# Cross-attention and mixture-of-experts kernel: operands over two queues, constants ahead, norms, weight pieces and first FFN chunks at other units

## What is computed

```
x = x + xattn(layernorm(x), ctx_1024)         # 16 heads of 8, causal mask, softmax
x = x + ffn(layernorm(x))                     # exact gelu
# xattn: q = Q @ Wq.T + bq, k and v from the context; w = softmax(mask(q @ k.T / sqrt(8)));
#        (w @ v) @ Wo.T + bo
# ffn:   shared experts (2 of 64) plus 16 routed experts of 64, top 4 of softmax(x @ router.T),
#        each gelu(x @ up.T) scaled by its gate, times down
```

## Time and profile before

| | us |
|---|---|
| median of 3 runs | 219.24 |
| lowest and highest of them | 218.1 and 220.63 |
| the profiled execution's own time | 219.43 |
| its span, first to last instruction | 217.7 |
| TensorE busy | 187.0 (86%) |
| VectorE busy | 170.6 (78%) |
| ScalarE busy | 143.4 (66%) |
| GpSimd busy | 97.1 (45%) |

### The profile page before, as it was taken

One profiled execution on the slowest core, in us unless ns is written; L12 is line 12 of the kernel. 1 busy time (PEld: TensorE's weight loads), 2 busy tenths in 40 slices (PEclk: granted clock), 3 DMA queues, 4 the chain that ended last, 5 costly groups with the idle time before them and its releaser, 6 DMA issues.

```text
span 217.7 us, 4911 instructions
## 1 busy us (share of the span) xinstructions
PE 187.0 (86%) x1610; PEld 137.3 (63%) x1610; DVE 170.6 (78%) x456; ACT 143.4 (66%) x285; POOL 97.1 (45%) x184
## 2 busy tenths in 40 slices
PE   0538689959999899999999997879959989999992
PEld 0316465646777577677767774457848758787871
DVE  4589969829689989999899994237788597787881
ACT  2261267746697687776766778866868977668661
POOL 5789018929569666566474666711112000000000
PEclk9999999996999999999999999999999999999999
DMA  4524332651332312312313200100000010010011
GB/s 121 168 62 121 77 102 78 212 155 52 93 87 51 103 56 63 106 39 77 79 53 81 74 5 5 32 6 24 3 2 0 5 50 0 0 48 0 9 41 48
DMA packets 23736, 12.98 MB, mean 60 GB/s; under 512 B 4696, under 2 KB 23400, under 8 KB 23712
## 3 DMA queue, kind: packets, MB, share of 16 engines
q1 hardware_dynamic: 23040, 12.52, 20.9%
q10 hardware_dynamic: 576, 0.13, 0.3%
q0 software_dynamic: 96, 0.03, 0.1%
HBM read 3.86 MB, written 1.05 MB: 23 GB/s over the span
## 4 chain that ended last, share of the span: by engine, by line
PE 50%; DVE 20%; issue 9%; SPq 8%; ACT 6%; DMA 3%; POOL 2%; POOLq 0%; DVEq 0%; ACTq 0%
DVE sb_mx L774 8%; SPq L335 6%; PE psum L964 6%; PE psum L946 4%; PE psum L883 3%; PE psum L880 3%; PE psum L881 3%; PE psum L923 3%; PE psum L865 3%; PE psum L867 3%; PE psum L866 3%; DVE sb_qk_res L757 2%; PE psum L872 2%; PE psum L967 2%; PE psum L930 2%
## 5 line engine op out<-in xcount | busy, mean ns | idle before, releaser
L774 DVE TENSOR_REDUCE sb_mx<-psum 128x2 f32<-128x512 f32 (+1 forms) x96 | 63.0, 679 | 8.0 <-PE psum L930 5.3
L582 ACT ACTIVATE sb_probs<-psum 128x512 f32<-128x512 f32 x96 | 55.9, 603 | 18.9 <-PE psum L946 18.0
L428 POOL TENSOR_SCALAR_AFFINE_SELECT sb_probs<-sb_probs 128x256 f32<-128x256 f32 (+1 forms) x96 | 45.1, 484 | 35.0 <-ACT sb_probs L582 34.4
L665 DVE TENSOR_TENSOR sb_probs<-sb_probs,psum 128x512 f32<-128x512 f32 x32 | 21.9, 684 | 10.1 <-ACT sb_probs L526 9.8
L526 ACT ACTIVATE sb_probs<-psum 128x512 f32<-128x512 f32 x36 | 21.4, 599 | 12.1 <-PE psum L867 12.0
L946 PE MATMUL psum<-sb_qk_op 128*128 128x256 bf16 x128 | 24.6, 274 | 3.1 <-ACT sb_probs L582 3.0
L923 PE MATMUL psum<-sb_qk_op 96*128 96x256 bf16 x128 | 25.9, 285 | 0.0
L672 DVE TENSOR_TENSOR sb_hid_l<-sb_probs,sb_hid_h 128x512 fp32r<-128x512 f32 x36 | 24.7, 685 | 0.3
L532 ACT CAST sb_hid_h<-sb_probs 128x512 fp32r<-128x512 f32 x36 | 22.2, 616 | 2.9 <-DVE sb_probs L665 2.9
L920 PE MATMUL psum<-sb_fut,sb_id_b 128*128 128x256 bf16 x64 | 18.3, 286 | 5.2 <-issue 4.4
L964 PE MATMUL psum<-sb_probs,sb_v_op 128*32 128x256 f32 x256 | 20.9, 398 | 0.8 <-ACT sb_o_raw L557 0.8
(11 more groups left out here) (114 smaller groups left out, 391.1 us busy)
## 6 DMA issues: line engine op xcount, KB each, us to landing
sb_qk_op<-sb_qk SPq DMA_DIRECT2D x96, 64.0 KB
sb_ctx<-in_ctx_t SPq DMA_DIRECT2D x8, 128.0 KB, 2.4
sb_num<-sb_o_raw SPq DMA_DIRECT2D x8, 128.0 KB, 2.1
out<-sb_o_raw SPq DMA_DIRECT2D x4, 256.0 KB, 2.3
sb_x<-in_x SPq DMA_DIRECT2D x3, 256.0 KB, 4.1
sb_up_f<-in_rup_t SPq DMA_DIRECT2D x1, 512.0 KB, 3.6
sb_dn_f<-in_rdown SPq DMA_DIRECT2D x1, 512.0 KB, 4.5
sb_x<-in_x SPq DMA_DIRECT2D x2, 128.0 KB, 3.5
```

The source lines that it names most:

```text
L428: nc.gpsimd.affine_select(out=v, in_=v, compare_op=ALU.is_ge, fill=0.0, base=0, pattern=[[0, v.shape[1]], [1, P]], channel_multiplier=-1). ...
L582: nc.scalar.activation(probs[g][:, u * BANK:(u + 1) * BANK], psum[:, BANK_S + n % SB, :], ACT.Exp, scale=float(DH) ** -0.5).then_inc(s_exp, 1)
L665: nc.vector.tensor_tensor(hid[buf[k]], gel[buf[k]], psum[:, 3 + k % 2, :], ALU.mult)\
L774: nc.vector.tensor_reduce(dst, src, AX, ALU.max).then_inc(m_max, 1)
```

## The change

- **Two queues.** The six transfers of half 1 of batch 0 are issued by ScalarE instead of SyncE: the first at unit 9 of turn 0, five after the projection of batch 1 at the end of turn 0. The wait on `m_ps` of batch 1's half 1 becomes 1 instead of 7.
- **Constants.** The seven constants are issued after part 2 of x and ahead of parts 3 and 4, in turn 0.
- **Zeros.** GpSimd's memsets stand in another order (those of `qk_op[0]` one after the other at the start, `spr` and `g_parts` at the end of turn 1), with counted `pads_set`; ScalarE's zeroing of half of `qk_op[1]` goes to its start and is written as 2048 f32 instead of 4096 bf16.
- **Norms.** `stats_1(4)` goes from the end of turn 0 to the end of turn 1; the norms, transposes and copies of parts 2, 3 and 4 go to units 4/7 of turn 1, 1/3 of turn 2 and 1/3 of turn 3, part 2 into a score bank, parts 3 and 4 into `BANK_B`. The fourth `add_bo` goes to unit 8 of turn 3.
- **Weight pieces.** Each is three units later: the first at unit 4 of turn 3, the eighth at unit 1 of turn 5.
- **FFN chunks.** `early_units` holds one more chunk in turn 9 (three), so that 18 instead of 17 stand in the turns, at other units.

The diff, cut to its core:

```diff
-        early_units = ((8, 10), (1, 2, 4, 6, 8, 10), (0, 1, 2, 4, 6, 7, 8, 9, 10))
+        early_units = ((8, 9, 10), (1, 2, 5, 7, 9, 10), (0, 1, 2, 4, 6, 7, 8, 9, 10))
...
         def weight_piece(turn, t, unit):
 
-            if turn.at not in (3, 4) or t % 3 != unit:
+            at = UNITS * (turn.at - 3) + t - 3
+            if not 0 <= at < 2 * UNITS or at % 3 != unit:
                 return None
...
-        xn_units = {(0, 9): 1, (1, 4): 2, (1, 7): 3, (1, 10): 4}
+        xn_units = {(0, 9): 1, (1, 7): 2, (2, 3): 3, (3, 3): 4}
+
+        xn_bank = (BANK_PV, SB + 2, BANK_PV, BANK_B, BANK_B)
...
                 if c == 1:
-                    sp.wait_ge(m_ps, UNITS // 2 * half + 1)
+                    sp.wait_ge(m_ps, 1)
...
+                    if (turn.at, t) == (0, 9):
+                        act.wait_ge(zeros_set[0], 2)
+                        act.wait_ge(qk_hi, 2)
+                        pairs(act, 0, 1, 0)
...
                 if turn.at == 0:
-                    zeros_1()
+                    act.wait_ge(qk_mid, 1)
+                    pairs(act, 0, 1, 1, 3, 4)
+                    act.wait_ge(qk_lo, 1)
+                    pairs(act, 0, 1, 2, 5)
...
-                    if isinstance(turn.at, int) and turn.at == 1 and t in (3, 6):
-                        apply_1(2 + t // 3)
+                    if (turn.at, t) in ((1, 4), (2, 1), (3, 1)):
+                        apply_1(turn.at + 1)
...
                 if turn.at == 0:
                     stats_1(3)
+                if turn.at == 1:
                     stats_1(4)
-                    apply_1(2)
-                if turn.at == 1:
                     dve.wait_ge(bv_ps, 1)
```

More of the change, by code:

```diff
@@ L359, in turn_of @@
                         sp.dma_start(dst[:, :], src).then_inc(mask_in, 16)
-                    for q in range(2, len(X_PARTS)):
-                        load_x(q)
-                c = turn.batch(1)
-                if c is not None:
-                    operands(c, turn.side(1), 1)
-                if turn.at == 1:
+                    load_x(2)
                     sp.wait_ge(pads_set, 1)
@@ L370, in turn_of @@
                         sp.dma_start(dst[:, :], src).then_inc(c_in, 16)
+                    load_x(3)
+                    load_x(4)
+                c = turn.batch(1)
+                if c is not None and c > 0:
+                    operands(c, turn.side(1), 1)
                 c = turn.batch(2)
```

83 lines of the change are left out of this document (42 added, 41 removed).

## The result

| | before | after |
|---|---|---|
| median of 20 runs each | 220.26 us | 222.68 us |
| profiled execution: time, span | 219.43, 217.7 | 223.47, 221.7 |

The ratio is 1.0113, with a 95% interval of 1.0078 to 1.0147. The forecast was 215.2, with a range of 213.0 to 218.2: wrong in size and in sign.

A forecast was written before the change was run, and what follows sets the result against it. It took VectorE and the operands to bound turn 1, SyncE's queue the chain from 9.7 to 29, and the weight wait turn 3. 219.43 - 3.6 - 0.4 = 215.4, for the median 215.2; range 213.0 to 218.2.

The forecast's parts named there:

- FFN chunks: Turns 9 to 11: extra chunk fills idle TensorE time, VectorE and gelu delays take some back; -0.4 us, between -1.6 and +1.0.
- all that stands ahead of them: Everything up to the start of turn 4, which was to come at 55.4: -3.6 us.
- Rival C: Turns 10 and 11: the attention comes later, +1.0 us instead of -0.4, total 216.6; chance 0.12.
- Weight pieces and turn 3: Turn 3: weight wait goes, sums become the next wait; reciprocal at 48.3 instead of 50.84, -2.5 us.
- The clock's price: Units behind turn 3's reciprocal: without the low clock, TensorE saves about 1.1 us.
- the norm of part 4 in turn 3: Turn 3: norm and transposes fall in VectorE's gaps and before the sums' landing; 0 us.
- Rival B: Turn 3: SyncE's queue holds the sums until 50.8; 219.0, no change, or half way 217; chance 0.13, whole or half.
- Start of the operands, 16.3: Before turn 1: cast of q and k at 0.43 us; TensorE starts at 16.3 instead of 17.25, about -1.0 us.
- Turn 1 and the first score, 28.5: Turn 1: VectorE again needs 11.4 us from its first reduction, at 17.1, so turn 2 starts at 28.5: -1.35 us.
- I keep the same stretch: Turn 1: TensorE's matmuls stay at the low clock level until about 21, as in the kernel before.
- Turn 2, +0.5: Turn 2: one norm on VectorE and four transposes on TensorE cost between 0 and 1.1 us; 0.5 taken.
- Rival D: Turn 2: TensorE stays at the low clock level, some 8 us longer, total 223; chance 0.04.

The follow-up runs named there:

- e3: The kernel before with nothing but the weight pieces three units later: 217.19 us, ratio 0.9870.
- e8: The kernel before with later weight pieces, two queues and cleared buffers in new places; norms and order of x and constants as before: 218.02 us, ratio 0.9880.
- e1: The changed kernel with the first FFN chunks back at their old units: 218.88 us, ratio 0.9931.
- e13: The changed kernel with the tail of e10 (chunk units and VectorE's order): 217.03 us, ratio 0.9897.
- e14: e8 with the tail of e10 (chunk units and VectorE's order): 215.75 us, ratio 0.9818.
- e7: e3 with the extra chunk in turn 9 and none at unit 0 of turn 11, 17 chunks: 217.77 us, ratio 0.9878.
- e5: e3 with turn 10's chunks alone at their new units, still 17 chunks: 217.96 us, ratio 0.9903.
- e6: e3 with the extra chunk in turn 9 alone, 18 chunks in all: 219.71 us, ratio 0.9983.
- e9: e1 with GpSimd's last two memsets at the end of turn 2 instead of turn 1: 218.53 us, ratio 0.9933.
- e4: e1 with the addition of `bo` ahead of `stats_1(4)` in VectorE's order at the end of turn 1: 219.19 us, ratio 0.9960.
- e10: e7 with VectorE's two instructions for the extra chunk behind the residual addition and statistics at the end of turn 9: 216.99 us, ratio 0.9863.

## Why the prediction was wrong

By ratios, the parts are: pieces -1.3% (e3), two queues +0.1% (e8 against e3), norms and loads +0.5% (e1 against e8) or +0.8% (e13 against e14), units +1.8% (after against e1). With +0.5% they add up to the measured +1.1%; they must, since each kernel is compared with the one before it in the chain, so the sum is no test of the parts. Only the pieces and the units are clear of the error; by the medians they are -1.4% and +1.7%. In the profiled executions, the changed kernel took 223.47 us and the forecast sum was 215.4. Of the 8.1 us between them, 5.7 are the chunks (-0.4 forecast, +5.3 measured) and 2.3 all that stands ahead of them (-3.6 forecast, -1.33 measured).

**FFN chunks, -0.4 us within -1.6 and +1.0: the step that failed.** It measured +5.3 us in the profile, with two stretches of low clock in it, and about +3.8 in the medians (222.68 against 218.88). The prediction saw one of the mechanisms, the two VectorE operations ahead of the residual addition (1.3 us; e7 has 1.2). It never walked the other moved chunks one by one to the thing that each stood in front of: the chunk at unit 4 of turn 10 covered the way of the transposes through ScalarE to the router (1.08 us idle in e5, its worth in the median small); the one at unit 4 of turn 11 had become the one that needs the last batch's inputs (1.08 us in e6, 1.84 in the changed kernel); and the chunk behind the turns covered the copy of the gates (0.87). Nor did it price what these gaps do to the clock. Its bounds were therefore those of one mechanism, not of the edit. Rival C had the sign, at a price of 1.0 instead of 4 to 5, and another mechanism: it put the delay ahead of the attention's division, where TensorE's waits in fact shrank to 0.32 and 0.17 us.

**Weight pieces and turn 3: right in mechanism, late through the terms ahead of it.** The wait vanished, the low clock of turn 3 with it, and den became the next wait. The clock's price was right (1.1 forecast, 1.0 in e3). The reciprocal came at 50.24 (predicted 48.3), because the sums were issued at 48.16 instead of 46.3; from there they took 2.1 us, as forecast. They went late since SyncE's queue began batch 2's half 0 at 35.16 instead of 33.4: turn 2 had itself begun 1.7 us late, and the queue handed that on. In e1, with the first score at 28.95, the reciprocal came at 48.74. What was put at nothing without a reason is the norm of part 4 in turn 3: behind the reciprocal, e1 takes 7.36 us to the output projection and e3 6.59, the meeting of VectorE and GpSimd above. Rival B was half true: den is the wait in e3 (1.06 us), but its landing did not stay at 50.8. In the medians, the change without its units gave 0.7%, some 1.5 us, of the 3.6 forecast for the head, and e3 alone 3.0.

**Start of the operands, 16.3: measured 16.65.** The cast was right (0.43). A term of -0.95 was -0.60, and that not in every execution: e9 and e4, with the same code up to there, start at 16.98 and 17.15.

**Turn 1 and the first score, 28.5: measured 30.21.** Two terms were mis-sized. `stats_1(4)` was counted as VectorE work in place of a norm, but it stands last in the turn, ahead of the addition of `bo` for which the first score waits. And "I keep the same stretch" at the slow rate failed: it lasted to 24.6 us or longer. e1 has the same head with the fast rate from 20.9 on, and its first score is at 28.95. So of the 1.7 us about 1.3 are the rate and 0.45 the rest. That the rate lasted that long in the one profile and not in the other is luck, on the bad side.

**Turn 2, +0.5: right in size by luck.** Turns 2 and 3 together cost 0.6 to 0.75 us more with the moved norms, but up to the reciprocal of turn 3 nothing; the cost stands behind it, where the prediction had 0. In the totals the moved norms cost 0.2 to 0.8%, by the pair of kernels and the measure; what of that exceeds the stretches is not located.

**Rival D** had the place wrong and the mechanism half right. TensorE stayed slow until 24.6 us or later, past the 22.5 that it named, but turn 2 was fast, and the price was 1.3 us and not 8. The Trainium skill (TensorE: Matmul & The Clock Gate, section "A second HAM failure mode: psum-queue depth-cycling") says that short idle times between groups of matmuls can make the clock swing. The tail of the changed kernel agrees, with two idle stretches of about 1 us ahead of the first fall; e6 does not, where three such stretches (0.98, 2.19 and 1.08) were followed by none.

## What to carry to other kernels

A filler is there for the wait that it covers. Before fillers are moved or one is added, list for each what stands behind it on TensorE and when that thing's inputs come, and list what the filler puts into the queues of the other engines, above all ahead of the additions and norms on which the next stage hangs. An idle stretch that is filled at one engine's expense is moved, not removed. Giving that engine the critical instruction first took the delay away in the profiles (e10, e14), though in the medians of e10 it can't be seen. And time the parts of a compound change apart: here one line, the later weight pieces, gained more than all the rest together, and a part that loses more than that was hidden beside it.
